# A one-core sandwich kernel: gathers and scatters of the expert rows at longer distances

## The chip, the cores and the metric

The kernel runs on one core of one Trainium2 chip. The metric is the device time of one execution in microseconds (us); the runs shown are summed up by their median. A core has five engines that the text names as the profile does: PE (TensorE; PEld is its weight load), DVE (VectorE), ACT (ScalarE), POOL (GpSimd) and SP (SyncE, which here only issues DMAs). The indirect DMAs, gathers and scatters with a list of row numbers, are issued by POOL.

## The reference

The input is x of 8 x 512 tokens of 128 numbers. Two blocks stand around it, each as x = x + layernorm(block(layernorm(x))). The first block is a Nystrom attention with a graph part (16,384 edges). The second, which the change touches, is a mixture of 16 experts, 4 of them for each token:

```
diff = x[:, :, None, :] - keys
logits = -sum(diff * diff) + x @ rw.T + rb            # [b, l, 16]
topv, topi = top_k(logits, 4);  w = softmax(topv)
hidden  = gelu(x @ w1[e].T + b1[e])                   # 128 -> 512, for each expert
exp_out = hidden @ w2[e].T + b2[e]                    # 512 -> 128
fused   = sum over the 4 chosen of w * exp_out
```

Everything is float32.

## The kernel before

**Stages.** The first 230 us or so of an execution are the attention, the graph part, the router logits of the first half of the tokens and their sorting. The rest is the expert stage. The 4096 tokens are 32 token tiles of 128, in two halves of TS = 16 tiles. Each token of a half appears four times, once for each chosen expert, so a half has JT = TS * TOPK = 64 *row tiles* of 128 rows, sorted by expert. A row tile can hold rows of more than one expert, so a half takes NI = 64 + 15 = 79 *steps*, each with one expert's weights; IALL = 158 steps in all, numbered 0 to 157. `step_of(n)` (L338) is the step of row tile n: n for the first half, n + 15 for the second (tile 64 is step 79).

**One step.** In step i, PE runs `up(i)` (L2135 to L2142: 8 matmuls, two for each of 4 chunks in float32), transposes the next row tile if one is due (`rows_T`, L2130 to L2133), then runs `down(i - 1)` (L2144 to L2150: 8 matmuls). ACT runs `gelu(i)` (L879 to L885: 4 activations), which waits for `up_ps`, the count that PE raises at the end of each `up`, and copies the transposed tile (L891). DVE runs `y_add(i - 2)` (L1657 to L1665), which waits for `down_ps` and raises `y_ready`, and for every fourth row tile `bring` (L1641 to L1655). SP loads the expert's weights (L462), four steps ahead at most.

**What POOL does in the expert stage.** For each row tile n, `rows(n)` (L585 to L594) gathers 128 rows from DRAM (L592), and `results(n)` (L596 to L602) scatters the finished tile of 128 rows to DRAM (L600): 128 gathers and 128 scatters, in one instruction order on one queue. A gather waits until `up` of the step NEAR = 8 before its own is done, and for its buffer (XR = 24 buffers, and the landing of the gather 12 before). A scatter of tile m waits for `y_ready` of step_of(m) + 16. The order is written out in L607 to L624: gather n first, from n = 27 on followed by scatter n - 27 (BEHIND); at the end of the first half scatters 37 to 50 alone; then gathers 64 to 76, each followed by scatter 51 to 63 (BEHIND_2 = 13); then gathers 77 to 90 alone; then from gather 91 on each followed by a scatter, 27 behind; at the end scatters 101 to 127. PE transposes tile n five steps before step_of(n), by `brought` (L345 to L348), except the first five tiles of the second half, 64 to 68, which are due at steps 72 to 76 and tile 69 at 79.

**The second half's row list.** Beside the steps of the first half, the second half's tokens are routed and sorted (`prepare` on DVE, ACT and PE). For each of its 16 token tiles DVE makes two one-hot tables (`tile_hots` L1456 to L1461, `lane_hots` L1463 to L1469), ACT one more (`hot_lanes` L819 to L825), and PE multiplies them (`table` L2067 to L2075) one step later. `hots_of(i)` (L351 to L353) says which token tile is due at step i: two in every three steps from step 44 to 67. At LIST_STEP = 69 DVE copies the finished list of row numbers from the PSUM (`row_list`, L1471 to L1474) and raises `idx_ready`, for which POOL waits ahead of gather 64. The same work for the first half is done ahead of the expert stage.

Of the kernel before, what the change touches and what calls it, by code (L numbers as in the profile page):

```python
# [5 lines left out]
def sandwich_kernel(nc, dense, adj_rows, adj_cols, adj_vals, wq, wk, wv_w, wv_b, qkv_w, wq_t, wk_t, out_w, out_b,  # L6
# [10 lines left out]
    P = 128  # L17
# [25 lines left out]
    TS = T // S  # L43
    JT = TS * TOPK
# [3 lines left out]
    RING = 8  # L48
    SLOTS = 32
    LEAD = 3  # L50
    BEHIND = 27
    GRP = 4
    XR = 24
    NEAR = 8
    XSEM = 12
    WR = 4
    BEHIND_2 = 13
# [5 lines left out]
    with ctx:  # L63
        def sb(name, shape, dt=fp32):
            return ctx.enter_context(nc.sbuf_tensor(name, shape, dt))

        def sem(name):
            return ctx.enter_context(nc.semaphore(name))
# [99 lines left out]
        kres = sb("kres", [P, NT, QK])  # L168
        ksp = sb("ksp", [P, NT, NS, QK], bf16)

        idx_i = sb("idx_i", [P, 2, EC], i32)
        idx_f = sb("idx_f", [P, 2, EC])
        neg = sb("neg", [P, EC])
# [145 lines left out]
        w1_in = [sem(f"w1_in{s}") for s in range(WR)]  # L319
        yk_in, pool_done = [sem(f"yk_in{i}") for i in range(3 + len(YCUTS) - 1)], sem("pool_done")  # L320
        out_ready, out_done = sem("out_ready"), sem("out_done")

        block = ctx.enter_context(nc.Block())

# [6 lines left out]
        def freed(eng, sem, count):  # L331

            if count > 0:
                eng.wait_ge(sem, count)
# [3 lines left out]
        def step_of(n):  # L338
            return n // JT * NI + n % JT
# [10 lines left out]

        def hots_of(i):  # L351
            j = i - HOT_STEP
            return TS + j // 3 * 2 + j % 3 if 0 <= j < 3 * TS // 2 and j % 3 < 2 else None  # L353

        HOT_STEP, LIST_STEP = 44, 69

# [32 lines left out]
        def act_lane(t):  # L389
            return t < LANES_ACT or t >= TS  # L390
# [17 lines left out]
        def hot_slot(t):  # L408
            return t if t < TS else t % HB[1]
# [88 lines left out]
        def _(pool):  # L498
# [83 lines left out]
                .then_inc(gates_ready, 1)  # L582


            def rows(n):  # L585
                if n >= NEAR:
                    pool.wait_ge(up_ps, step_of(n) - NEAR + 1)
                if n >= XR:
                    pool.wait_ge(own_ready, 3 * ((n - XR) // GRP) + 1)
                if n >= XSEM:  # L590
                    pool.wait_ge(xg_in[n % XSEM], 16 * (n // XSEM))
                pool.indirect_dma_start(out=xg[:, n % XR, :], out_offset=None, in_=xd[n // JT][:, :],  # L592
                                        in_offset=bass.IndirectOffsetOnAxis(ap=idx_src[:, n:n + 1], axis=0))\
                    .then_inc(xg_in[n % XSEM], 16)  # L594

            def results(m):  # L596
                pool.wait_ge(y_ready, step_of(m) + E)
                if m >= RING:
                    pool.wait_ge(y_out[m % RING], 16 * (m // RING))
                pool.indirect_dma_start(out=yd[:, :],  # L600
                                        out_offset=bass.IndirectOffsetOnAxis(ap=idx_dst[:, m:m + 1], axis=0),
                                        in_=yg[:, m % SLOTS, :], in_offset=None).then_inc(y_out[m % RING], 16)  # L602
# [1 line left out]
            pool.wait_ge(pool_done, POOL_PRE)  # L604
            pool.wait_ge(idx_ready, 1)
            pool.wait_ge(xd_done, 16)
            for n in range(JT):  # L607
                rows(n)
                if n >= BEHIND:
                    results(n - BEHIND)  # L610
            for m in range(JT - BEHIND, JT - BEHIND_2):
                results(m)
            pool.wait_ge(idx_ready, 2)
            pool.wait_ge(xd_done, 32)
            for n in range(JT, JT + BEHIND_2):
                rows(n)
                results(n - BEHIND_2)
            for n in range(JT + BEHIND_2, JT + BEHIND):
                rows(n)
            for n in range(JT + BEHIND, JALL):  # L620
                rows(n)
                results(n - BEHIND)
            for m in range(JALL - BEHIND, JALL):
# [299 lines left out]
        def _(dve):  # L923
# [342 lines left out]
            def some_stats(src, t0, t1, last):  # L1266
                for t in range(t0, t1):
                    ins = v.bn_stats(stats[:, t, :], src[:, t, :])
                step(ins)
                for t in range(t0, t1):  # L1270
                    ins = v.bn_aggr(mv[:, t, :], stats[:, t, :])  # L1271
                if last:
                    ins.then_inc(stat_ready, 1)
# [182 lines left out]
            def tile_hots(t0, n):  # L1456
                h, s = t0 // TS, hot_slot(t0)
                v.tensor_tensor(out=hot_tile[h][:, s:s + n, :, :].rearrange("p a k n -> p (a k) n"),
                                in0=iota_r[:, 0:JT].unsqueeze(1).broadcast_to([P, n * TOPK, JT]),
                                in1=tile_of[:, t0 % TS:t0 % TS + n, :].rearrange("p t k -> p (t k)").unsqueeze(2)  # L1460
                                .broadcast_to([P, n * TOPK, JT]), op=ALU.is_equal).then_inc(hot_ready, 1)  # L1461

            def lane_hots(t):  # L1463
                h, s = t // TS, t % HB[t // TS]
                freed(dve, hot_used, t - HB[h] + 1)
                for k in range(TOPK - act_lane(t)):
                    ins = v.tensor_scalar(hot_lane[h][:, s, k, :], iota_r[:, 0:P], lane[:, t % TS, k:k + 1],  # L1467
                                          code[:, t:t + 1], ALU.is_equal, ALU.mult)
                ins.then_inc(hot_ready, 1)  # L1469
# [52 lines left out]
            def normal(to, of, t, last):  # L1522
                ins = v.tensor_scalar(to, of, rstd[:, t:t + 1], nmr[:, t:t + 1], ALU.mult, ALU.add)
                if t % NT == NT - 1:
                    ins.then_inc(last, 1)

            def prepare(i):
                if 25 <= i < 25 + TS:
                    normal(xrow[:, i - 25, 0:D], x[:, TS + i - 25, :], TS + i - 25, xn_ready)
                if 1 <= i <= 6:  # L1530
                    t = TS + min(3 * (i - 1), 12 + 2 * (i - 5))
                    some_stats(xn, t, t + (3 if i < 5 else 2), i == 6)
                elif 7 <= i <= 9:
                    root(1, i - 7, 3, EPS / 4)
                elif i == 10:
                    shifts(1)
                elif 11 <= i <= 19:
                    t = TS + 2 * (i - 11)
                    if i < 19:
                        second_x(t, t + 2)  # L1540
                    if i > 11:
                        some_stats(x, t - 2, t, i == 19)
                elif 20 <= i <= 22:
                    root(1, i - 20, 4, EPS)
                elif i == 24:
                    norm_2(1)
                    square_norm(1)
                    logits_1(1)
                elif i == 25:
                    logits_2()  # L1550
                elif i == 26:
                    logits_3(1)
                elif i == 27:
                    highest()
                elif i == 28:
                    lowered()
                    highest_at(0, 4)
                elif i in (29, 30):
                    highest_at(4 + 6 * (i - 29), 10 + 6 * (i - 29))
                elif i == 31:  # L1560
                    step(v.tensor_copy(topf[:, 0:TS, :], topi[:, :, 0:TOPK]))
                    one_hots(0, 2)
                elif i == 32:
                    one_hots(2, TOPK)
                elif i == 33:
                    chosen_experts()
                elif i == 34:
                    dve.wait_ge(chosen_ready, 2)
                    dve.wait_ge(xd_done, 16)
                    targets(1)  # L1570
                elif i == 36:
                    counts(1)
                elif i == 37:
                    starts()
                elif i in (38, 39):
                    position_1(2 * (i - 38), 2 * (i - 37))
                elif i in (40, 41):
                    position_2(2 * (i - 40), 2 * (i - 39))
                elif i == 42:
                    lanes_and_tiles()  # L1580
                elif i == HOT_STEP + 2:
                    gates_1(1)
                elif i == HOT_STEP + 5:
                    gates_2(1)
                elif i == HOT_STEP + 8:
                    after_start()
                elif i == HOT_STEP + 11:
                    experts_of(1)
                elif i == HOT_STEP + 14:
                    step_experts()  # L1590
                elif i == HOT_STEP + 17:
                    expert_row(1)
                elif i == LIST_STEP:
                    row_list(1)
                if hots_of(i):
                    tile_hots(hots_of(i), 1)
                    lane_hots(hots_of(i))


            def finish(i):  # L1600
# [625 lines left out]
```

## Time and profile before

| what | value |
|---|---|
| median of 3 runs | 700.9 us (699.55 to 707.57) |
| span of the profiled execution | 694.4 us |
| PE busy | 536.4 us, 77% |
| POOL busy | 281.1 us, 40% |
| ACT busy | 353.7 us, 51% |
| DVE busy | 364.9 us, 53% |
| first gather starts | 229.56 us into the span |
| last scatter starts | 664.6 us into the span |

The span runs from the first to the last instruction of one profiled execution; its own device time is not shown apart, so the 6.5 us between the span and the median of the runs stand for what lies around it. The busy shares are means over stages with different limits: in the first 230 us POOL is mostly idle, in the expert stage it issues the indirect DMAs.

### The profile page before, as it was taken

Reading aid. Unit: us, or ns where it says so; the run is one execution under the profiler, and the core shown is the slowest. Engines: PE = TensorE matmul, PEld = TensorE weight load, DVE = VectorE, ACT = ScalarE, POOL = GpSimd, SP = SyncE. Lnnn points to the kernel's source line nnn. Section 1 sums busy time; section 2 is a strip of 40 time slices with the busy share of each in tenths; the row PEclk is TensorE's granted clock in tenths of the full one; section 3 lists DMA queues with packets and bytes.
Section 4 is the critical chain, followed back from the end, with each engine's and each line's share of the span. In section 5 each row is a group of like instructions: output and inputs, shape, how many; then the busy total and the mean of one; then the engine's idle time right before and its main releaser. Section 6 shows DMA issues by size and latency. Waiting matters only on the chain.

```text
span 694.4 us, 19926 instructions
## 1 busy us (share of the span) xinstructions
PE 536.4 (77%) x6242; PEld 481.6 (69%) x6242; DVE 364.9 (53%) x1325; ACT 353.7 (51%) x1079; POOL 281.1 (40%) x308
## 2 busy tenths in 40 slices
PE   4999879994502789977678789789977776679984
PEld 4967779993401489976677679678967776668942
DVE  6554779997999356545434553112334432233126
ACT  6524167775556365546445667336634434335513
POOL 4000000000451543566666743664566666645520
PEclk9999999998655799999999999999999989989998
DMA  8970000006001455444444645445866644546553
GB/s 229 255 280 9 3 3 0 0 0 243 1 1 76 120 161 157 138 131 131 131 140 143 204 124 162 135 144 146 264 207 180 183 130 133 145 122 192 174 197 122
DMA packets 55746, 92.28 MB, mean 133 GB/s; under 512 B 10352, under 2 KB 26096, under 8 KB 55152
## 3 DMA queue, kind: packets, MB, share of 16 engines
q1 hardware_dynamic: 45424, 72.35, 35.0%
q0 software_dynamic: 10240, 18.89, 9.2%
q8 instruction: 44, 0.72, 0.4%
q14 instruction: 38, 0.31, 0.1%
HBM read 78.07 MB, written 17.37 MB: 137 GB/s over the span
## 4 chain that ended last, share of the span: by engine, by line
PE 43%; issue 18%; DVE 18%; POOL 8%; ACT 7%; DMA 2%; DVEq 2%; another core or an unknown queue 0%; POOLq 0%; SPq 0%; ACTq 0%
PE bank L2148 15%; PE bank L2141 13%; POOL yd L600 6%; ACT value L883 3%; DVE shared L1187 2%; DVE shared L1179 2%; POOL shared L592 2%; DVE early L1467 2%; PE bank L1735 2%; DMA shared<-yd 1%; PE bank L1772 1%; PE bank L1840 1%; PE bank L1762 1%; PE bank L2133 1%; PE bank L2089 1%
## 5 line engine op out<-in xcount | busy, mean ns | idle before, releaser
L883 ACT ACTIVATE value<-bank,shared 128x128 f32<-128x128 f32 x632 | 180.8, 376 | 203.0 <-PE bank L2141 156.7
L2148 PE MATMUL bank<-shared,value 128*128 x1264 | 182.7, 290 | 62.4 <-ACT value L883 41.7
L2148 PEld LDWEIGHTS bank<-shared,value 128*128 128x128 f32 x1264 | 161.7, 200 | 76.7 <-issue 76.1
L2141 PE MATMUL bank<-early,shared 128*128 x1264 | 180.9, 288 | 5.3 <-issue 2.8
L592 POOL DMA_INDIRECT shared<-xd,early x128 | 125.5, 980 | 127.5 <-PE bank L2141 79.8
L2141 PEld LDWEIGHTS bank<-early,shared 128*128 128x128 f32 x1264 | 162.6, 200 | 9.3 <-issue 8.4
L1663 DVE SCALAR_TENSOR_TENSOR early<-bank,value,early 128x128 f32 x158 | 55.4, 351 | 195.8 <-PE bank L2148 116.6
L600 POOL DMA_INDIRECT yd<-early x128 | 128.3, 1002 | 67.8 <-DVE early L1663 36.2
L560 POOL TENSOR_TENSOR shared<-shared,xn 128x512 f32<-128x512 f32 x4 | 5.1, 1264 | 174.9 <-DVE xn L1262 167.1
L2133 PE MATMUL bank<-ident,shared 128*128 128x128 f32 x128 | 35.9, 284 | 9.0 <-DMA shared<-xd,early 5.7
L2003 PE MATMUL bank<-ksp,shared 128*128 128x32 bf16 x1536 | 40.9, 177 | 0.0
L2003 PEld LDWEIGHTS bank<-ksp,shared 128*128 128x128 bf16 x1536 | 40.0, 96 | 0.1
L891 ACT ACTIVATE early<-bank 128x128 f32<-128x128 f32 x128 | 38.4, 304 | 2.5 <-PE bank L2133 2.0
L2013 PE MATMUL bank<-xnT,shared 128*128 128x96 bf16 x512 | 24.3, 206 | 7.2 <-DVE xnT L1206 7.2
L1741 PE MATMUL bank<-zeros 128*128 128x512 bf16 x61 | 17.3, 444 | 15.0 <-DVE mv L1271 13.0
L1645 DVE TENSOR_TENSOR value<-shared,mask 128x128 f32<-128x128 f32 x16 | 4.7, 292 | 45.9 <-PE bank L2133 40.7
L2013 PEld LDWEIGHTS bank<-xnT,shared 128*128 128x128 bf16 x512 | 22.4, 98 | 8.4 <-issue 6.2
L2133 PEld LDWEIGHTS bank<-ident,shared 128*128 128x128 f32 x128 | 18.9, 148 | 11.9 <-DMA shared<-xd,early 7.4
L1187 DVE TENSOR_SCALAR shared<-iota_r,idx_f 128x512 bf16<-128x512 f16 x90 | 24.9, 345 | 0.4 <-PE bank L2013 0.4
L1179 DVE TENSOR_SCALAR shared<-shared,iota_c 128x1024 bf16 x56 | 23.3, 478 | 0.0
L1741 PEld LDWEIGHTS bank<-zeros 128*128 128x128 bf16 x61 | 6.4, 109 | 23.7 <-DVE mv L1271 13.1
L753 ACT ACTIVATE xnT<-iota_r,idx_f 128x512 f16<-128x512 f16 x32 | 21.1, 707 | 0.0
(334 smaller groups left out, 689.3 us busy)
## 6 DMA issues: line engine op xcount, KB each, us to landing
shared<-w1b SPq DMA_DIRECT2D x158, 258.0 KB
w1b<-in_w_t SPq DMA_DIRECT2D x1, 4096.0 KB, 17.8
shared<-col_dram SPq DMA_DIRECT2D x1, 4096.0 KB, 13.4
shared<-in_w_t SPq DMA_DIRECT2D x1, 4096.0 KB, 12.3
att<-yd SPq DMA_DIRECT2D x8, 512.0 KB
shared<-yd SPq DMA_DIRECT2D x4, 1024.0 KB, 9.1
xd<-xnT SPq DMA_DIRECT2D x2, 1280.0 KB
shared<-xd,early POOLq DMA_INDIRECT x128
```

The lines of the kernel that those rows point to most:

```text
L592: pool.indirect_dma_start(out=xg[:, n % XR, :], out_offset=None, in_=xd[n // JT][:, :], in_offset=bass.IndirectOffsetOnAxis(ap=idx_src[:, ...
L600: pool.indirect_dma_start(out=yd[:, :], out_offset=bass.IndirectOffsetOnAxis(ap=idx_dst[:, m:m + 1], axis=0), in_=yg[:, m % SLOTS, :], in_ ...
L883: ins = act.activation(hT[:, i % 2, tok(c)], bank[2 + i % 2][:, tok(c)], ACT.Gelu, bias=w1_now[:, i % WR, F + c:F + c + 1])
L891: act.activation(xgT[:, n % SLOTS, :], bank[n % 2][:, 0:P], ACT.Copy).then_inc(xgT_ready, 1)
L1179: ins = v.tensor_scalar(oh_c[:, s, c, :], colb[:, bass.ds(g * (EG * P), EG * P)], iota_c[:, c:c + 1], None, ALU.is_equal)
L1187: ins = v.tensor_scalar(oh_r[:, s, j, :], iota_r[:, :], idx_f[:, 0, bass.ds(g * EG + j, 1)], None, ALU.is_equal)
L1663: v.scalar_tensor_tensor(out=y, in0=bank[6 + i % 2][:, 0:P], scalar=own_f[:, bass.ds(at * (2 * E) + e, 1)], in1=y, op0=ALU.mult, op1=ALU.a ...
L2003: ins = mm(bank[s][:, j * QK:(j + 1) * QK], oh_c[:, s, c, j * P:(j + 1) * P], ksp[:, c, n, :], start=(c == 0 and n == 0), stop=(c == NT - ...
L2013: ins = mm(bank[4][:, c * NS * QK:(c + 1) * NS * QK], oh_r[:, s, j, tok(c)], kvs[:, s, j, :, :].rearrange("p n q -> p (n q)"), start=False ...
L2133: nc.tensor.transpose(bank[n % 2][:, 0:P], xg[:, n % XR, 0:D], ident[:, :]).then_inc(xgT_ps, 1)
L2141: ins = mm(bank[2 + i % 2][:, tok(c)], w1_now[:, i % WR, tok(c)], x_now, start=True, stop=True)
L2148: ins = mm(bank[6 + i % 2][:, 0:D], hT[:, i % 2, tok(c)], w2_sb[:, bass.ds(e, 1), c, :] .rearrange("p a d -> p (a d)"), start=(c == 0), st ...
```

## The change

Six things are changed, and nothing of what is computed:

1. NEAR goes from 8 to 16: a gather waits for the `up` of the step 16 before its own.
2. BEHIND goes from 27 to 34: scatters stand 34 gathers behind in the order.
3. A `pause` is added: POOL writes a scratch tile (`pause_to`, 128 x 64 float32) with a memset and waits for the memset's own semaphore. It stands behind each gather that has no scatter behind it: gathers 0 to 33 and 77 to 97.
4. The loop over the first half's gathers is written as two loops, which for the order of gathers and scatters is the same as before but for the value of BEHIND.
5. The second half's one-hot tables are made at one token tile a step, steps 44 to 59, with the lane tables ahead of the tile tables on DVE.
6. `row_list(1)` moves from step 69 to step HOT_STEP + TS + 2 = 62. LIST_STEP itself stays 69 and still sets `brought`, the steps at which PE transposes.

```
-    BEHIND = 27
+    BEHIND = 34
-    NEAR = 8
+    NEAR = 16
+        pause_to = sb("pause_to", [P, P // 2])
+        paused = sem("paused")
         def hots_of(i):
             j = i - HOT_STEP
-            return TS + j // 3 * 2 + j % 3 if 0 <= j < 3 * TS // 2 and j % 3 < 2 else None
+            return TS + j if 0 <= j < TS else None
+            def pause():
+                pool.memset(pause_to[:, :], 0.0).then_inc(paused, 1)
+                pauses[0] += 1
+                pool.wait_ge(paused, pauses[0])
-            for n in range(JT):
+            for n in range(BEHIND):
                 rows(n)
-                if n >= BEHIND:
-                    results(n - BEHIND)
+                pause()
+            for n in range(BEHIND, JT):
+                rows(n)
+                results(n - BEHIND)
 ...
             for n in range(JT + BEHIND_2, JT + BEHIND):
                 rows(n)
+                pause()
 ...
-                elif i == LIST_STEP:
+                elif i == HOT_STEP + TS + 2:
                     row_list(1)
                 if hots_of(i):
+                    lane_hots(hots_of(i))
                     tile_hots(hots_of(i), 1)
-                    lane_hots(hots_of(i))
```

## Rows read from the trace of the kernel before

**Rows 1.** The page's line of busy time, share of the span and instructions of each engine.
```profile
PE 536.4 (77%) x6242; PEld 481.6 (69%) x6242; DVE 364.9 (53%) x1325; ACT 353.7 (51%) x1079; POOL 281.1 (40%) x308
```

**Rows 2.** Stretches, `up` matmuls alone (x8 a step): start:end, length, busy, clock, DMA share, GB/s.
```profile
237.80:282.30 44.50, 20.59 (x152) 18.44 (x152) 1.00 0.55 148
282.30:372.10 89.80, 35.20 (x240) 31.56 (x240) 0.94 0.47 135
372.10:409.90 37.80, 15.20 (x96) 12.80 (x97) 0.95 0.54 165
409.90:429.80 19.90, 11.13 (x80) 9.76 (x81) 1.00 0.56 158
429.80:473.40 43.60, 17.07 (x120) 15.63 (x121) 0.96 0.49 143
473.40:498.30 24.90, 12.70 (x96) 11.78 (x96) 1.00 0.69 200
498.30:586.70 88.40, 35.10 (x240) 31.78 (x241) 0.92 0.61 177
586.70:622.70 36.00, 12.49 (x80) 11.43 (x81) 0.91 0.45 129
622.70:661.00 38.30, 21.46 (x160) 19.42 (x160) 1.00 0.61 172
```

**Rows 3.** The same view for POOL: busy time and instructions in two of the stretches.
```profile
282.30:372.10 89.80, 58.32 (x58) 0.94 0.47 135
473.40:498.30 24.90, 11.82 (x13) 1.00 0.69 200
```

**Rows 4.** Timeline of steps 39 and 40: start, length, engine, line, idle before and releaser.
```profile
341.15 1.06 PE L2141 MATMUL bank<-early,shared 128*128 x8
341.66 0.97 POOL L592 DMA_INDIRECT shared<-xd,early  x1 [0.30 <-issue]
342.94 1.49 POOL L600 DMA_INDIRECT yd<-early  x1 [0.30 <-issue]
344.97 1.14 ACT L883 ACTIVATE value<-bank,shared 128x128 f32<-128x128 f32 x4 [3.60 <-remote]
345.20 0.97 POOL L592 DMA_INDIRECT shared<-xd,early  x1 [0.78 <-PE bank L2141]
```

**Rows 5.** Timeline of step 93, with gathers alone.
```profile
488.83 1.06 PE L2141 MATMUL bank<-early,shared 128*128 x8
489.93 1.14 ACT L883 ACTIVATE value<-bank,shared 128x128 f32<-128x128 f32 x4 [0.59 <-PE bank L2141]
490.16 0.98 POOL L592 DMA_INDIRECT shared<-xd,early  x1 [0.95 <-PE bank L2141]
```

**Rows 6.** Timeline of ACT and DVE at a one-hot table of the second half.
```profile
419.58 0.99 DVE L1467 TENSOR_SCALAR xnT<-iota_r,att,code 128x128 f16<-128x128 f16 x3
420.52 0.42 ACT L822 ACTIVATE xnT<-iota_r,att 128x128 f16<-128x128 f16 x1
420.97 0.49 ACT L824 ACTIVATE xnT<-xnT,code,ncode 128x128 f16<-128x128 f16 x1
```

**Rows 7.** Timeline at step 72: gather 64 and the transpose of tile 64.
```profile
431.77 0.99 POOL L592 DMA_INDIRECT shared<-xd,early  x1 [6.79 <-issue]
435.46 0.33 PE L2133 MATMUL bank<-ident,shared 128*128 128x128 f32 x1 [2.77 <-DMA shared<-xd,early]
```

**Rows 8.** Timeline of the start: the last gather of the first burst, and `gelu(1)`.
```profile
240.35 0.95 POOL L592 DMA_INDIRECT shared<-xd,early  x1 [0.30 <-issue]
242.96 1.14 ACT L883 ACTIVATE value<-bank,shared 128x128 f32<-128x128 f32 x4 [2.42 <-PE bank L2141]
```

**Rows 9.** POOL's timeline: a memset waited for, what follows it, and the first gather.
```profile
0.81 0.20 POOL L506 MEMSET ident<- 128x128 f32 x1 [0.29 <-POOLq L2219]
1.26 0.28 POOL L507 TENSOR_SCALAR_AFFINE_SELECT ident<-ident 128x128 f32<-128x128 f32 x1 [0.24 <-POOL ident L506]
229.56 1.73 POOL L592 DMA_INDIRECT shared<-xd,early  x1 [13.04 <-issue]
```

More of the change, by code:

```diff
@@ L582, in _ @@
                 .then_inc(gates_ready, 1)
+            pauses = [0]
+            def pause():
+                pool.memset(pause_to[:, :], 0.0).then_inc(paused, 1)
+                pauses[0] += 1
+                pool.wait_ge(paused, pauses[0])
             def rows(n):
```

## The prediction

> **What bounds the kernel now.** The first thing to read is that no engine is full: PE is busy for 77% of the span and POOL for 40% [rows 1]. So I cut the expert stage into stretches by what POOL does in them, and counted steps by the `up` matmuls, 8 to a step [rows 2]. The nine stretches hold 19, 30, 12, 10, 15, 12, 30, 10 and 20 steps, 158 together, and cost per step:
>
> - gathers alone (steps 0 to 18): 44.5 / 19 = 2.34 us; the second half's (86 to 97): 24.9 / 12 = 2.08;
> - a gather and a scatter each step (19 to 48): 89.8 / 30 = 2.99; in the second half (98 to 127): 88.4 / 30 = 2.95;
> - the end of such a phase and the scatters left over from it (49 to 60): 37.8 / 12 = 3.15; in the second half (128 to 137): 36.0 / 10 = 3.60;
> - scatters alone (61 to 70): 1.99; (138 to 157, with the tail): 1.92;
> - the boundary of the halves (71 to 85): 43.6 / 15 = 2.91.
>
> PE has the same 16 matmuls in each step. What makes a step one microsecond dearer is that gathers and scatters stand together. The next view shows how [rows 4]. `up(39)` ends at 341.15 + 1.06 = 342.21, but ACT, which waits for PE's counts alone, starts its gelu at 344.97, and POOL's next gather, which waits for the same count, is released at 345.20. PE's count reaches the others 2.8 us late. Meanwhile POOL runs gather and scatter with 0.30 us between them; the count comes 0.5 us after the scatter (342.94 + 1.49 = 344.43) ends. Where POOL idles 0.95 us between gathers, gelu follows `up` by 489.93 - 489.89 = 0.04 us [rows 5]. I call this a *hold*: while POOL issues indirect DMAs back to back, what PE has finished is made known late. Its cause I can't read; that it goes with unbroken runs I can. A pair takes 0.97 + 0.30 + 0.99 + 0.30 = 2.56 us of POOL [rows 4], more than the 2.08 us of a step with gathers alone, so runs stay unbroken until POOL has to wait for PE. Over 30 steps POOL is busy 58.3 of 89.8 us, against 11.8 of 24.9 without scatters [rows 3].
>
> **The change, part by part.** Its sum is made against the span of 694.4 us and the 6.5 us between it and the median of 700.9; the profiled execution's own device time is not shown, so I take it as the median.
>
> *Distances.* A gather with its number n may go once `up(n - 16)` is done, a scatter behind it once `y_add(n - 19)` is. So gather 34 with scatter 0 goes at step 19, and the phase of pairs is steps 19 to 48 (gathers 34 to 63) in place of about 20 to 56, and 98 to 127 (gathers 98 to 127) in place of 99 to 135: 30 pairs twice where there were 37. All 128 gathers and 128 scatters remain. The 14 pairs that are parted turn into scatters alone.
>
> *Steps 49 to 60* (37.8 us before). Ten of them (49 to 58) still transpose a tile and now always make a one-hot table. ACT then has 1.14 (gelu), 0.3 (copy of the tile) and 0.42 + 0.49 [rows 4, 6], 2.35 us less small overlaps: I take 2.3. DVE's three lane tables of 0.99 [rows 6] and its other work of the step stay below that by about as much. Two steps without either are 1.9. Leftover scatters: at the last pair only about two are due, against four or more before, since the gather's wait stood 7 steps ahead and the scatter's 11, and now 15 and 18. I allow 2.5 us for one last hold. Sum: 23.0 + 3.8 + 2.5 = 29.3, gain **8.5**.
>
> *Steps 61 to 85* (19.9 + 43.6 = 63.5 before). Gather 64 stands behind scatter 50, which needs `y_add(65)`, and behind the row list, now copied at step 62. So it starts near step 68, not at the release of 72, and tile 64 is transposed at step 72: about 4 steps between, where there was none. Before, PE waited 2.77 us for it, 3.7 us after its issue [rows 7], and for tiles 66 to 68 less each. But thirteen pairs stay, and the hold with them: 13 x 2.95 = 38.4; the other 12 steps at 1.9 to 2.0, 23.1. Sum 61.5, gain **2.0**. The row list moves past one POOL wait only; the second half's rows are stored by SP at step 56, as before, and its weight loads keep their waits.
>
> *Steps 86 to 127.* As before, but step 98 now has a pair: **-1.0**.
>
> *Steps 128 to 137* (36.0 before). Scatters alone, 10 x 1.92 = 19.2, and 2.5 for the last hold: 21.7, gain **14.3**.
>
> *Pauses.* 55 of them. A memset and its wait take 1.26 - 0.81 = 0.45 us from start to start [rows 9]; the tile written here is half as wide. A gather so takes about 1.25 + 0.35 = 1.6 us of POOL. In a step with gathers alone POOL idles 0.95 us [rows 5], which hides it. Not hidden is the start: 16 gathers may now go without a wait from PE, where 8 did. Bounds: about nothing, if the pauses break the run (the eighth gather comes 7 x 0.35 = 2.5 us later, and the hold up to 242.96 [rows 8] falls away); or a hold until the burst ends. Before, the ninth gather started at 240.35 and gelu(1) at 242.96, 2.6 later [rows 8]; gather 15 would start at 229.6 + 2.4 + 14 x 1.6 = 254.4 [rows 9], so gelu(1) at 257: 14 us later. I take zero, since a broken run is nearer to [rows 5], and keep 14.
>
> *One-hot tables at one a step*: the tables themselves are counted above; after step 60 the old ones fall away (inside the 1.9). The order lane before tile on DVE: both are counted before the matmul starts, nothing. Scratch tile, semaphore: nothing.
>
> Sum: 8.5 + 2.0 - 1.0 + 14.3 = 23.8. Span 670.6, **time 677 us**.
>
> **The skill against it.** The trace shows a gather stretched to 1.73 us [rows 9] and a scatter to 1.49 [rows 4], where 0.97 to 0.99 is usual. The Trainium skill, SBUF — State Buffer, section "SBUF: two separate sides", calls the port pair of GpSimd and VectorE an exclusive lock: the pauses' writes could then wait for a DVE operation, or hold one up. That speaks against the pauses; no row shows such a wait of a memset in the expert stage. The rule for the dear pause below is in the Trainium skill too, GPSIMD Engine Reference, section "Instruction dispatch": an instruction completes when all eight cores are done, and this gates only who waits for its semaphore. By it a pause ends with the gather's descriptors and not with its landing, which would strike the last rival out; no row here shows it.
>
> **The rivals.**
>
> *POOL becomes the bound and the hold shrinks.* With eight more steps of lead the pairs could run at 2.56 us: 73 pairs x 0.39 = 28 us more, 649 us. Against it: POOL catches up with its waits whatever the lead is, and then has to wait for PE again.
>
> *The start is held.* 14 us as above, and up to 4 more where gathers 77 to 81 become free together near step 81: 691 to 695 us. For it: gelu(1) was late behind a burst already [rows 8].
>
> *The pause is dear.* If each gather behind a memset took the 1.73 us of the first one [rows 9], a gather would need 2.7 us, more than a step. Gather 33 would land, 3.7 us after its issue [rows 7], near 229.6 + 33 x 2.7 + 3.7 = 322.4; tile 33 is due at step 28, now at 282.3 + 9 x 2.99 = 309.2 [rows 2]: 13 us. In the second half 21 gathers take 56.7 us where the 25 steps until tile 97 is due take about 49: 8 us. 698 us.
>
> *The pause waits for the landing; the one on the slower side.* Then a gather with its pause takes 3.7 [rows 7] + 0.4 = 4.1 us. First half 33 x 4.1 + 229.6 + 3.7 - 309.2 = 59, second 21 x 4.1 - 49 = 37: 773 us at the most. It decides for slower from 54 t - 125 = 31, which is t = 2.9 us for a gather and its pause. Against it: memsets in the trace end in 0.2 us and are waited out in 0.24 more; but none stands behind an indirect DMA.
>
> **How the numbers follow.** A change of 1% (7 us) is about what can be told from none: 693.9 and 707.9. Forecast 0.66, POOL bound 0.05, start held 0.14, pause dear 0.07, waiting for the landing 0.08. Half of the held start ends near 695 and counts within 1%, as does the dear pause: faster 0.78, same 0.14, slower 0.08. The forecast's own range is 662 to 690 (last holds of 0 to 5 us each, ACT's 2.3 between 2.0 and 2.6, the boundary's gain 0 to 7). The range over the cases is 660 to 698; it leaves out 649 and what lies beyond 698.
>
> **What would show it.** After the change gathers and scatters should stand together in 73 steps at 2.9 to 3.0 us, and steps 49 to 60 and 128 to 137 should cost 2.2 to 2.5; PE's waits for gather 64 should be gone; gather-to-gather distance in the first burst about 1.6 us. If gelu(1) starts after 250, the start is held. If PE waits for gathers around step 28, the pause is dear. The forecast is wrong in its core if scatters alone, now earlier, cost 3 us a step too.

## The result, and the profile after

The changed kernel takes 709.7 us (705.7 to 717.9, 19 runs) where the kernel before takes 701.6 (699.5 to 707.6, 19 runs): a ratio of 1.0111, with a 95% interval of 1.0086 to 1.0137. It is slower by 8 us; 677 was forecast. The profiled execution has a span of 707.9 us against 694.4, 13.5 more; a second trace of the same kernel (`f1_after_b` below) has 702.7, so some of these 13.5 us belong to the one execution. The trace of the kernel before is also a quick one: in every run of the record that lists both, the span is 1.7 to 2.0 us shorter than the device time, not 6.5, so that execution took about 696 us, some 5 below the median (an estimate from these spans).

The page of the changed kernel, its busy line, to lay beside [rows 1]:

```profile
PE 539.5 (76%) x6240; PEld 489.0 (69%) x6242; DVE 364.1 (51%) x1325; ACT 355.5 (50%) x1079; POOL 291.4 (41%) x363
```

The work is the same but for 55 memsets on POOL (308 instructions became 363). Time went into waits, so the stretches have to be compared. These are the changed kernel's, cut at the same steps and with the same columns as [rows 2]:

```profile
237.50:293.10 55.60, 21.43 (x152) 19.29 (x152) 0.91 0.47 131
293.10:385.30 92.20, 35.17 (x240) 31.83 (x240) 0.94 0.46 133
385.30:419.40 34.10, 14.21 (x96) 12.16 (x96) 0.95 0.52 162
419.40:443.20 23.80, 11.51 (x80) 10.71 (x81) 0.87 0.56 156
443.20:497.10 53.90, 18.70 (x120) 17.64 (x121) 0.80 0.41 116
497.10:521.60 24.50, 12.67 (x96) 11.74 (x96) 1.00 0.67 201
521.60:612.90 91.30, 35.81 (x240) 32.40 (x241) 0.93 0.59 173
612.90:637.30 24.40, 11.57 (x80) 10.53 (x80) 0.93 0.53 149
637.30:676.00 38.70, 21.32 (x160) 19.46 (x160) 1.00 0.63 180
```

Five rows moved by more than 3 us. Steps 0 to 18 cost 55.6 us instead of 44.5, steps 61 to 85 cost 23.8 + 53.9 = 77.7 instead of 63.5, and against that steps 49 to 60 gave 3.7 back and steps 128 to 137 gave 11.6. Where 11 us went in the first row, the changed kernel's timeline says (start, length, engine, line, what it did, idle time before it and who ended it; lines are picked here and in the timelines below):

```profile
241.54 1.09 PE L2153 MATMUL bank<-early,shared 128*128 x8
...
243.86 0.17 POOL L590 MEMSET pause_to<- 128x64 f32 x1
244.23 1.08 PE L2153 MATMUL bank<-early,shared 128*128 x8
244.30 0.95 POOL L601 DMA_INDIRECT shared<-xd,early  x1 [0.27 <-POOL pause_to L590]
245.69 0.95 POOL L601 DMA_INDIRECT shared<-xd,early  x1 [0.27 <-issue]
...
252.10 1.14 ACT L895 ACTIVATE value<-bank,shared 128x128 f32<-128x128 f32 x4 [9.14 <-remote]
...
255.43 0.95 POOL L601 DMA_INDIRECT shared<-xd,early  x1 [0.27 <-issue]
257.64 1.91 PE L2153 MATMUL bank<-early,shared 128*128 x8
258.05 1.14 ACT L895 ACTIVATE value<-bank,shared 128x128 f32<-128x128 f32 x4 [3.52 <-remote]
```

The first line is `up(2)`; it ends at 242.63. ACT, which waits for PE alone, starts `gelu(2)` at 252.10, 9.5 us later. `up(3)` ends at 245.31 and `gelu(3)` starts at 258.05, 12.7 us later; `up(4)`, which stands behind `down(2)` and so behind `gelu(2)`, starts only at 257.64. All that time POOL issues gathers 1.39 us apart (0.95, the memset's 0.17, 0.27 of waiting), 19 of them from 229.6 to 255.4. I call such a row of indirect DMAs, with at most a pause between two of them, a *run*, and NEAR, the number of steps that a gather may be ahead, its *lead*: this is the run that the lead of 16 allows. Step 3 takes 13.4 us. The same again at the boundary, where gathers 77 to 81 follow the last pair:

```profile
475.50 1.06 PE L2153 MATMUL bank<-early,shared 128*128 x8
476.72 0.99 POOL L601 DMA_INDIRECT shared<-xd,early  x1 [0.30 <-issue]
477.39 1.06 PE L2153 MATMUL bank<-early,shared 128*128 x8
477.70 0.18 POOL L590 MEMSET pause_to<- 128x64 f32 x1
478.15 0.97 POOL L601 DMA_INDIRECT shared<-xd,early  x1 [0.27 <-POOL pause_to L590]
...
482.34 0.95 POOL L601 DMA_INDIRECT shared<-xd,early  x1 [0.27 <-issue]
484.41 1.14 ACT L895 ACTIVATE value<-bank,shared 128x128 f32<-128x128 f32 x4 [8.63 <-remote]
```

This is `gelu(81)`, 484.41 - 476.56 = 7.9 us behind the end of `up(81)` (the first line), and it starts 1.1 us after the last gather of the run has ended (483.29). Steps 69, 77 and 82 take 6.1, 8.3 and 10.5 us. The granted clock of the stretch is 0.80, between the two levels of 1.2 and 2.4 GHz, where it was 0.96 [rows 2]; PE's `up` is busy for 18.7 us instead of 17.1, so the waits are the larger part.

### The profile page after: what moved, and what is told of

Its sections match the earlier page's. It is cut to its first block, busy times and chain, and to the rows that moved or that the text cites. A ratio compares the mean times of both kernels' runs of the same rounds, so it can differ in the third digit from the quotient of the medians.

```text
span 707.9 us, 20013 instructions
## 1 busy us (share of the span) xinstructions
PE 539.5 (76%) x6240; PEld 489.0 (69%) x6242; DVE 364.1 (51%) x1325; ACT 355.5 (50%) x1079; POOL 291.4 (41%) x363
## 3 DMA queue, kind: packets, MB, share of 16 engines
q1 hardware_dynamic: 45424, 72.35, 34.7%
## 4 chain that ended last, share of the span: by engine, by line
PE 38%; DVE 18%; issue 17%; POOL 8%; another core or an unknown queue 7%; ACT 7%; DVEq 3%; DMA 2%; POOLq 0%; SPq 0%; ACTq 0%
PE bank L2160 13%; PE bank L2153 10%; POOL yd L609 6%; ACT value L895 2%; DVE shared L1199 2%; DVE shared L1191 2%; DVE early L1479 2%; POOL shared L601 2%; DMA shared<-yd 1%; PE bank L1747 1%; DVE early L1675 1%; DVEq L1675 1%; PE bank L1852 1%; PE bank L1784 1%
## 5 line engine op out<-in xcount | busy, mean ns | idle before, releaser
L2160 PE MATMUL bank<-shared,value 128*128 x1264 | 187.6, 295 | 72.7 <-ACT value L895 43.8
L2160 PEld LDWEIGHTS bank<-shared,value 128*128 128x128 f32 x1264 | 167.3, 206 | 84.9 <-issue 84.2
L2153 PEld LDWEIGHTS bank<-early,shared 128*128 128x128 f32 x1264 | 165.8, 204 | 6.6 <-issue 6.1
L609 POOL DMA_INDIRECT yd<-early x128 | 130.2, 1017 | 89.8 <-DVE early L1675 65.0
L765 ACT ACTIVATE xnT<-iota_r,idx_f 128x512 f16<-128x512 f16 x32 | 21.1, 707 | 0.0
```

Of the source, the lines that this page charges most:

```text
L609: pool.indirect_dma_start(out=yd[:, :], out_offset=bass.IndirectOffsetOnAxis(ap=idx_dst[:, m:m + 1], axis=0), in_=yg[:, m % SLOTS, :], in_ ...
L2153: ins = mm(bank[2 + i % 2][:, tok(c)], w1_now[:, i % WR, tok(c)], x_now, start=True, stop=True)
L2160: ins = mm(bank[6 + i % 2][:, 0:D], hT[:, i % 2, tok(c)], w2_sb[:, bass.ds(e, 1), c, :] .rearrange("p a d -> p (a d)"), start=(c == 0), st ...
```

## The experiments

**Two levels.** The same two kernels do not always stand in this relation. In some comparisons the kernel before takes 699 to 702 us and in others 642 to 645, with all kernels of one comparison on the same level. I call the first *held* and the second *free*, for in the free ones PE's counts are not late anywhere: in all eight free traces no gelu starts more than 0.5 us after its `up` has ended and ACT is free, and in each of the twelve held ones 37 to 58 of the 158 do. One chip number came up with both levels, so I can't say what the level belongs to. The result above is a held one. The expectations of `e1_nopause` to `e4_ramp` were written before the free level was known, for the held one, and those four runs came out free; what they say of the held level is tested by later runs. Ratios are only compared within a level, and this table of stretches (us, from the starts of `up`) is read the same way; sum is steps 0 to 156.

```
steps      before after f1   f2   f3   f4   e6    e8   g3   g4   h1  | free: e3   a1
0-3          9.8  20.0 20.3 21.1  8.8  8.9  22.8  8.8 13.1  8.8  9.6 |      8.8   8.8
4-18        34.7  35.5 35.2 33.9 34.9 34.8  34.1 39.1 40.7 42.7 34.8 |     34.9  35.2
19-33       43.5  46.2 46.2 44.3 55.7 37.9  59.9 47.8 46.2 44.8 44.7 |     34.7  35.0
34-48       46.3  46.0 45.9 47.4 47.6 47.9  49.2 47.2 45.9 47.4 47.1 |     42.4  35.9
49-60       37.7  34.1 31.6 31.3 30.1 48.0  34.4 29.0 31.8 31.6 40.4 |     33.4  28.3
61-70       20.0  23.9 21.4 22.6 21.5 19.7  20.6 22.1 18.5 18.5 18.5 |     18.0  18.0
71-85       43.6  53.9 55.1 53.5 50.2 44.3  59.1 45.9 45.6 44.4 45.6 |     38.7  30.4
86-97       24.9  24.5 24.5 24.5 24.5 24.6  24.5 30.7 37.3 34.3 24.6 |     25.5  24.8
98-127      88.4  91.3 92.2 91.8 93.7 84.7 107.3 94.2 91.2 91.2 93.4 |     74.3  63.9
128-137     36.0  24.4 24.1 25.9 24.6 43.9  27.6 26.0 24.5 26.3 35.9 |     25.0  22.5
138-156     37.1  36.0 34.2 36.1 34.7 36.0  38.6 34.8 34.9 34.8 36.0 |     34.3  34.8
sum          422   436  431  432  426  431   478  425  430  425  431 |      370   338
```

**The changed kernel itself, twice more.** `a1_after` and `f1_after_b` are the changed kernel, unedited.

> The changed kernel itself, unaltered, beside the kernel before, for comparison with the four variants. Where PE's counts are not held back during POOL's bursts (gelu 0.04 us behind up in the steps of pairs), theory A expects it faster than before by 3 to 4%: the bursts are harmless, pairs cost some 2.4 us a step. Where they are held back (gelu 2 to 3 us behind up in the steps of pairs of the kernel before), it is slower by about 1%, with 12 us lost at the start and 10 near step 82.

Measured, free: 612.4 us against 645.5, ratio 0.9529 (0.9444 to 0.9613), more than the 3 to 4% that was expected there. Its busy line and three of its stretches (steps 0 to 18, 19 to 48, 98 to 127):

```profile
PE 510.8 (84%) x6242; PEld 463.6 (76%) x6242; DVE 363.9 (60%) x1325; ACT 357.7 (59%) x1079; POOL 288.8 (47%) x363
```

```profile
238.50:282.50 44.00, 21.94 (x152) 19.84 (x153) 0.96 0.59 164
282.50:353.40 70.90, 32.94 (x240) 29.11 (x240) 1.00 0.61 171
...
454.90:518.80 63.90, 32.64 (x241) 29.21 (x242) 1.00 0.80 237
```

POOL runs the very same burst at the start, and here nobody waits for it. Its timeline:

```profile
245.15 0.95 POOL L601 DMA_INDIRECT shared<-xd,early  x1 [0.27 <-POOL pause_to L590]
245.43 1.06 PE L2153 MATMUL bank<-early,shared 128*128 x8
246.53 1.14 ACT L895 ACTIVATE value<-bank,shared 128x128 f32<-128x128 f32 x4 [0.53 <-PE bank L2153]
246.54 0.95 POOL L601 DMA_INDIRECT shared<-xd,early  x1 [0.27 <-POOL pause_to L590]
```

The gelu follows `up` by 246.53 - 246.49 = 0.04 us in the middle of the burst. So every hold read here stands beside a run of indirect DMAs, but a run does not make a hold by itself. In the free trace the 30 steps of the pairs cost 70.9 us, 2.36 each, though a pair still takes POOL 2.56: PE draws on the lead of 16 while POOL falls behind. With the lead of 8 that reserve ends half way (`e3_hots`, 34.7 and then 42.4 us for 15 steps each).

> The changed kernel itself, beside its own variants. Two regimes are known by now: on some chips PE's counts reach the others at once and the kernel before takes 642 to 645 us; on others they are held back while POOL issues indirect DMAs close together, and it takes 699 to 702. Where they are held: ratio 1.00 to 1.02, with steps 0 to 3 at 20 us and one step of about 10 us near step 82. Where they are not: ratio 0.95, as measured there once (612.4 against 645.5).

Measured, held: 710.8 us against 701.0, ratio 1.0143 (1.0063 to 1.0224); steps 0 to 3 took 20.3 us, step 83 took 8.5. The first result repeats.

**The pauses.** `e1_nopause`, `e5_nopause_b` and `f2_nopause_c` are the changed kernel without them:

```diff
             for n in range(BEHIND):
                 rows(n)
-                pause()
...
             for n in range(JT + BEHIND_2, JT + BEHIND):
                 rows(n)
-                pause()
```

> The changed kernel without its 55 pauses behind gathers. Theory A (what counts is how closely the indirect DMAs follow each other, and for how many): the start's gathers come 1.25 us apart instead of 1.39, still held; steps 0 to 3 take 18 to 20 us and the boundary as long as with pauses or 1 to 2 us less, ratio to the kernel before 1.00 to 1.02. Rival B (a pause's wait is itself what lets the counts be held, a semaphore more in the same queue): steps 0 to 3 fall to 10 us, ratio 0.98. Rival C (the pause does break the hold in part): steps 0 to 3 over 22 us and the steps 4 to 18 longer, ratio 1.03. On a chip that holds nothing: 0.95, as measured (611.1).

Measured: held 712.1 us, ratio 1.0167 (1.0089 to 1.0244), steps 0 to 3 at 21.1 us, a little over the 18 to 20 of theory A. Free: 610.3, 0.9519 (0.9404 to 0.9634), and, beside `a1_after`, 611.1, 0.9503 (0.9416 to 0.9589). The pauses do nothing that can be measured at either level; `e5_nopause_b`, for which 1 to 2% over the changed kernel was expected at the free level, is 0.2% faster. Theory A (the spacing of the indirect DMAs and their number decide) stands: 1.25 us between gathers is held like 1.39. Doubled pauses, `e2_pause2` and `f3_pause2_b` (`pause()` twice in each place):

> The changed kernel with each pause doubled: gathers come about 1.83 us apart where nothing else is waited for. Theory A by spacing: if 1.83 us between two indirect DMAs is enough for PE's counts to get through, steps 0 to 3 fall from 20 us to under 12 and the singles stay as they are, 10 us below the changed kernel (ratio about 0.99 to 1.00 where counts are held). Rival (the hold ends only when POOL has nothing left to issue for about a microsecond): steps 0 to 3 last 16 gathers of 1.83 us, 24 to 27 us, ratio 1.02 or more. On a chip that holds nothing: 0.985, as measured (634.7).

Measured: held 706.5 us, ratio 1.0082 (1.0038 to 1.0126); free 634.7, 0.9854 (0.9743 to 0.9966). Its timeline at the start:

```profile
246.11 0.38 POOL L590 MEMSET pause_to<- 128x64 f32 x2
246.75 0.95 POOL L601 DMA_INDIRECT shared<-xd,early  x1 [0.27 <-POOL pause_to L590]
247.91 1.06 PE L2155 MATMUL bank<-early,shared 128*128 x8
248.36 0.95 POOL L601 DMA_INDIRECT shared<-xd,early  x1 [0.27 <-issue]
249.01 1.14 ACT L897 ACTIVATE value<-bank,shared 128x128 f32<-128x128 f32 x4 [0.53 <-PE bank L2155]
```

At 1.60 us between gathers (248.36 - 246.75) the gelu is 249.01 - 248.97 = 0.04 us behind: no hold, and steps 0 to 3 fall from 20.0 to 8.8. But these slower gathers have not reached the lead of 16 when the pairs begin. POOL then runs 14 indirect DMAs with no break, and steps 25 and 26 take 11.5 and 8.0 us: steps 0 to 33 sum to 99.4 us against 101.7 with single pauses and 88.0 before. The hold moved, and the 10 us that theory A expected to gain came to 4.3 (706.5 for 710.8).

**One-hot tables and list.** `e3_hots` is the kernel before with only this part of the change:

```diff
-            return TS + j // 3 * 2 + j % 3 if 0 <= j < 3 * TS // 2 and j % 3 < 2 else None
+            return TS + j if 0 <= j < TS else None
...
-                elif i == LIST_STEP:
+                elif i == HOT_STEP + TS + 2:
...
+                    lane_hots(hots_of(i))
                     tile_hots(hots_of(i), 1)
-                    lane_hots(hots_of(i))
```

> The kernel before with the one-hot tables at one token tile a step and the row list at step 62 alone; distances and pauses as before. If the denser tables are near free beside the steps of pairs: 700 to 703 us. If they cost what a hold hides in part (ACT and DVE are fuller in steps 44 to 59): 705 or more. The earlier row list can't release gather 64, which then still waits for step 72.

Measured, free: 644.7 us, ratio 1.0043 (0.9993 to 1.0093): no difference that can be told, though not at the level that the expectation was written for. `e7_oldlist` takes the same part back from the changed kernel:

> The changed kernel with its one-hot tables and its row list as before (two in three steps, list at step 69). It tells what the earlier list is worth. Gather 64 then waits for step 69 in place of some step 68: if the boundary's gain comes from the gather's distance, it is within 0.5% of the changed kernel; if it comes from the list, 1 to 2% slower than that.

Measured, held: 711.2 us, ratio 1.0170 (1.0118 to 1.0223); its steps 49 to 60 took 29.8 us, no longer than the 29 to 34 with the denser tables, and its steps 61 to 85 took 80.1, against 77.7 and 76.5 in the two held traces of the changed kernel. Its ratio is above their 1.0111 and within the interval of their 1.0143, each from another comparison. No worth of this part shows at either level.

**The lead alone.** `e6_near16` is the kernel before with `NEAR = 16` for 8:

> The kernel before with NEAR at 16 and nothing else: 16 gathers free at the start, scatters still 27 behind, the row list still at step 69. The scatters' own wait then bounds the pairs. Where PE's counts are held back during POOL's bursts (gelu 2 to 3 us behind up in the steps of pairs), theory A expects a loss of 8 to 12 us at the start, so 1% slower or more. Where they are not, it expects a little gain, since gather 64 no longer waits for step 72: 0 to 1%.

Measured, held: 744.9 us, ratio 1.0664 (1.0599 to 1.0729), the worst of all, 46 us where 8 to 12 were expected. Steps 128 to 137 fall to 27.6, but the start costs 22.8, with one step of 15.7, and steps of 6 to 11 us stand all along the pairs. Its timeline at the boundary:

```profile
458.44 1.06 PE L2141 MATMUL bank<-early,shared 128*128 x8
461.16 0.98 POOL L592 DMA_INDIRECT shared<-xd,early  x1 [0.30 <-issue]
462.45 0.97 POOL L600 DMA_INDIRECT yd<-early  x1 [0.30 <-issue]
...
466.30 0.98 POOL L592 DMA_INDIRECT shared<-xd,early  x1 [0.31 <-issue]
468.98 1.40 ACT L883 ACTIVATE value<-bank,shared 128x128 f32<-128x128 f32 x5 [8.96 <-remote]
```

A run of nine indirect DMAs, the first four of them before 461.16, and `gelu(71)` 468.98 - 459.50 = 9.5 us late.

**The scatters' distance alone.** `f4_behind34` is the kernel before with `BEHIND = 34` for 27:

> The kernel before with BEHIND 27 made 34 and nothing else: NEAR stays 8, no pauses, old one-hots, row list at 69. It keeps the part of the change that takes pairs away and leaves out the longer lead of the gathers, which by the theory is what makes POOL issue 16 gathers unbroken at the start and after the boundary. Expected where counts are held: steps 0 to 3 at 10 us as before, 49 to 60 shorter by 4 to 8 us, 128 to 137 shorter by about 11, boundary unchanged: 680 to 688 us, ratio 0.97 to 0.98. Rival (the gain at 128 to 137 comes from the longer lead and not from the scatters' distance): ratio 0.995 to 1.00. On a chip that holds nothing the singles with lead 8 take 2.1 to 2.4 us a step as the pairs' 2.5 fall away for 7 steps twice: ratio 0.99.

Measured, held: 714.8 us, ratio 1.0197 (1.012 to 1.0275). The main expectation, 680 to 688, failed, and the rival named for it holds. Fewer pairs do help while they last (steps 19 to 33: 37.9 for 43.5), but at their end the lead of 8 leaves 34 - 8 = 26 steps between last gather and its scatter instead of 19, and the scatters left over go in one run. Its timeline:

```profile
397.16 0.97 POOL L600 DMA_INDIRECT yd<-early  x1 [0.30 <-issue]
398.93 1.06 PE L2141 MATMUL bank<-early,shared 128*128 x8
...
407.38 0.97 POOL L600 DMA_INDIRECT yd<-early  x1 [0.30 <-issue]
407.49 0.37 PE L2141 MATMUL bank<-early,shared 128*128 x1 [1.02 <-issue]
408.93 0.37 PE L2141 MATMUL bank<-early,shared 128*128 x1 [1.06 <-issue]
...
410.51 1.14 ACT L883 ACTIVATE value<-bank,shared 128x128 f32<-128x128 f32 x4 [6.18 <-PE bank L2141]
```

Nine scatters stand in this run, and `gelu(57)` is 410.51 - 399.99 = 10.5 us late. PE itself is late here: the eight matmuls of `up(58)`, between which the program has no wait, take 5.3 us (from 404.97) instead of the usual 1.1 to 2.1. `up(54)` of `h1_near12` below shows the same, 4.4 us. Scatters alone hold too: steps 49 to 60 cost 48.0 us and 128 to 137 cost 43.9. The changed kernel gains at these two places with lead and distance together (34 - 16 = 18). The distance alone loses there; the lead alone (`e6_near16`, 27 - 16 = 11) gains 3.3 and 8.4 us there and loses more elsewhere.

**Raising the lead gently.** `e4_ramp` and `e8_ramp_mid16` are the changed kernel with a lead that climbs from 8 to 16 over the single gathers (e4: with lead 8 for the 13 paired gathers of the boundary; e8: with 16 there):

```diff
-                if n >= NEAR:
-                    pool.wait_ge(up_ps, step_of(n) - NEAR + 1)
+                if n >= 8:
+                    pool.wait_ge(up_ps, step_of(n) - lead(n) + 1)
```

> The changed kernel with the lead of the gathers grown from 8 to 16 over gathers 8 to 34 and 77 to 98, and 16 for gathers 64 to 76. Where counts are held, theory A expects both bursts' holds gone, 20 us less than the changed kernel (680 to 692 us where before is 701). Where they are not, it is within 1% of the changed kernel, and 1 to 2% faster than the same ramp with a lead of 8 for gathers 64 to 76 (0.975 of before).

Measured: e4 free 625.8 us, ratio 0.9748 (0.9646 to 0.985); e8 held 704.0, 1.0071 (1.0029 to 1.0114), where 680 to 692 was expected. The 13 us step is gone (8.8 for steps 0 to 3), and against the kernel before 4.4 us come back in steps 4 to 18 and 5.8 in steps 86 to 97, where each pair of gathers close together is held. Steps 61 to 85 take 68.0 us although the 13 paired gathers keep the lead of 16: 4.5 more than before, where the changed kernel, whose gathers 77 to 81 follow at once, takes 14.2 more.

**Wider spacing by a little.** `g1_gap156` and `g3_gap156_b` are one kernel, `g2_gap173` and `g4_gap173_b` another: the changed kernel with pauses of two or three memsets and one wait, and lead 8 for the boundary's 13 paired gathers.

```diff
-                pool.memset(pause_to[:, :], 0.0).then_inc(paused, 1)
+                pool.memset(pause_to[:, 0, :], 0.0)
+                pool.memset(pause_to[:, 1, :], 0.0).then_inc(paused, 1)
...
-                if n >= NEAR:
-                    pool.wait_ge(up_ps, step_of(n) - NEAR + 1)
+                near = 8 if JT <= n < JT + BEHIND_2 else NEAR
+                if n >= near:
+                    pool.wait_ge(up_ps, step_of(n) - near + 1)
```

> The changed kernel with two edits: each pause is two memsets and one wait (gathers alone come about 1.56 us apart instead of 1.39, where 1.83 let PE's counts through at the start and 1.39 held them), and the 13 gathers that are paired with scatters at the boundary keep the old lead of 8. Theory A (spacing and number of indirect DMAs in a row decide): if 1.56 is enough, steps 0 to 3 take 9 to 12 us, the lead has reached 16 before the pairs begin, so steps 19 to 33 stay at 46 (not 56 as with 1.83), and steps 71 to 85 fall from 54 to 44 to 47: 10 to 18 us under the changed kernel, ratio to the kernel before 0.975 to 0.995 where counts are held. Rival (1.56 still holds): steps 0 to 3 take 20 to 23 us and only the boundary gains, ratio 1.00 to 1.01. On a chip that holds nothing: 0.955 to 0.975.

> The same with three memsets to a pause (1.73 us), beside it. Where counts are held: steps 0 to 3 at 9 us, one unbroken run of 4 to 8 us in steps 22 to 26, boundary 44 to 47, ratio 0.98 to 1.00. Where they are not: 0.976, as measured.

The spacings came out at 1.48 and 1.56 us, not 1.56 and 1.73. Only g2's ratio fell into the range that theory A had for it. Free (g1, g2): 626.6 and 626.2 us, ratios 0.9775 (0.9743 to 0.9807) and 0.9764 (0.9735 to 0.9793); the lead of 8 costs 9 us at steps 71 to 85 there (39.4 and 39.7 against 30.4). Held (g3, g4): 708.8 and 702.8 us, ratios 1.0137 (1.0079 to 1.0196) and 1.0044 (1.0002 to 1.0087). At the start the hold came later and in smaller parts: steps 0 to 18 took 53.8 and 51.5 us, against 55.5 in the changed kernel and 44.5 before, and `gelu(3)` of g4 is 2.8 us late between gathers 1.56 us apart. The boundary's pairs are as before (45.6 and 44.4), so a lead of 8 for these 13 gathers takes their loss away, but the gathers behind them now raise the lead from 8 to 16 and are held in steps 86 and 87 (9.9 and 7.4 us in g3, 7.8 and 6.6 in g4). Steps 68 to 97 sum to 88.8 and 84.6 us, against 89.7 and 88.3 in the two traces of the changed kernel. The hold moved again and shrank by 4 to 5 us at most.

**A smaller lead.** `h1_near12`: doubled pauses, `NEAR = 12`, lead 8 in the boundary's pairs.

> The changed kernel with doubled pauses, NEAR 12 in place of 16, and lead 8 for the boundary's 13 paired gathers. Theory A (raising the lead costs a hold unless the gathers come 1.6 to 1.9 us apart, and it has to be raised before the pairs begin): by steps, where counts are held, 0 to 18 at 44, 19 to 48 at 91 with no unbroken run at step 25 (a lead of 12 is reached by gather 34, 16 was not), 49 to 60 at 33, 68 to 97 at 78, 98 to 127 at 91, 128 to 137 at 29, the rest as before: 414 against 422 before, ratio 0.985 to 0.993, the first below the kernel before. Rival (the gains at the ends of the pairs need the full lead of 16): 49 to 60 at 38 and 128 to 137 at 35, ratio 1.00 to 1.01. On a chip that holds nothing: 0.98 to 0.99.

Measured, held: 707.3 us, ratio 1.0073 (1.0037 to 1.0108), not 0.985 to 0.993. Up to step 48 the expectation holds (136.2 us against 134.3 before, no burst at step 25). The ends do not: steps 54 and 132 take 11.4 and 11.6 us, and the stretches cost 40.4 and 35.9 us, as the rival had it. POOL's timeline around step 54:

```profile
385.35 0.97 POOL L602 DMA_INDIRECT shared<-xd,early  x1 [1.50 <-remote]
386.62 1.11 POOL L610 DMA_INDIRECT yd<-early  x1 [0.30 <-issue]
...
395.83 0.97 POOL L610 DMA_INDIRECT yd<-early  x1 [0.30 <-issue]
400.38 1.01 POOL L610 DMA_INDIRECT yd<-early  x1 [3.58 <-DVE early L1678]
```

The last gather of the half is followed by eight scatters with no break, the ones left over by a distance of 34 with a lead of 12. Step 132 has the same with seven. Step 107 takes 10.5 us in a third way: doubled pauses have set the gathers 1.97 us apart while a step takes 1.90, so the lead has not grown when the pairs begin, and POOL runs ten indirect DMAs unbroken.

No version beats the kernel before where it is held. Where it is free the changed kernel does, by 4.7%, and so does it without its pauses.

## Why the prediction was wrong, step by step

**The hold itself** was read correctly from [rows 4, 5], and it decides the result. What failed is that I took it for a property of single pairs and charged each stretch for the pairs in it. The runs showed a delay that goes with the whole of a run of POOL, and a longer lead makes the runs longer.

**Pauses and start, taken as zero**: this is the step that failed first. "A broken run is nearer to [rows 5]" chose the wrong end. [Rows 5] has 0.95 us of idle POOL between gathers; a pause leaves 0.44 from gather to gather, 0.17 of it the memset. The start, a term put at nothing, cost 10.2 us (steps 0 to 3, 20.0 for 9.8), inside the bound of 14 that I kept, at 1.39 us between gathers where I forecast 1.6. Removing the pauses changed nothing, doubling them ended this hold: shown by f2 and f3. The sign named for it, `gelu(1)` after 250, was the wrong one: `gelu(1)` started at 240.46 and `gelu(2)` at 252.10.

**Steps 61 to 85, forecast 61.5 us**: measured 77.7. This is the largest error, 16 us. I counted thirteen pairs at the 2.95 of before, though their gathers' lead rises from 8 to 16 in this place too: POOL runs up to six indirect DMAs of the pairs in a row, and then gathers 77 to 81 as well. The prediction had up to 4 us for the latter in a rival and nothing for the former. g3 and g4, whose pairs with lead 8 cost what they did before, show that the lead is the cause. How the 14.2 us lost divide is less sure: `e8_ramp_mid16` keeps the lead of 16 in the pairs, parts only the gathers behind them, and loses 4.5.

**Steps 49 to 60, forecast 29.3**: measured 34.1, and 31.6 in the second trace. The mechanism is right, the last hold was larger than 2.5 us in the first trace (step 49 took 6.4).

**Steps 86 to 127, forecast -1.0**: -2.5. **Steps 128 to 137, forecast 21.7**: 24.4, a gain of 11.6 for 14.3. I had put it down to parted pairs; `f4_behind34` shows that these alone lose 7.9 us here, and `h1_near12`, with a lead of 12, gains 0.1, while the longer lead without parted pairs (`e6_near16`) gains 8.4: most of the gain is the lead's.

**The one-hot tables at nothing**: right, by e3 and e7. **The boundary's late gather**: this part came as forecast and still gained nothing. Gather 64 starts at 433.46, in step 68, and PE transposes its tile at 446.32 without a wait. But the next gelu starts only at 448.11, after 5.1 us of idle ACT, and step 72 takes 5.0 us as before: a hold stands where the wait for the gather stood.

Of the rivals *the start is held* came true, with 0.14 and 691 to 695 us; with the 16 us of the boundary added to its 691 it would have given 707. *The pause is dear* and *the pause waits for the landing* did not happen: a gather behind a memset took 0.95 us, and the pair of both 1.39. The 2.7 us for a gather in the first of them is also wrong by its own rows: 1.73 in place of 0.97 makes 1.6 into 2.4, and its 698 us into about 680. The Trainium skill, GPSIMD Engine Reference, section "Instruction dispatch", ties the completion of an instruction to the work of all eight cores. This trace agrees: the next gather starts 0.44 us after the last one has ended, memset and wait between them, while 3.7 us lay between a gather's start and the first use of its rows [rows 7]. The Trainium skill's SBUF — State Buffer, section "SBUF: two separate sides", spoke against the pauses by the port shared with VectorE; no run shows such a wait, the 55 memsets took 0.163 to 0.177 us each. *POOL becomes the bound* gave 649 us for the changed kernel, from pairs at 2.56 us. Where nothing is held it takes 612.4, its pairs 2.36 us each; that the kernel before takes 642 to 645 there, near 649, is chance.

The sum (us, seen from the kernel before; minus is a loss): steps 0 to 48 forecast 0, measured -13.4; 49 to 60 8.5 and 3.6; 61 to 85 2.0 and -14.2; 86 to 127 -1.0 and -2.5; 128 to 137 14.3 and 11.6; 138 to 156 0 and 1.1. Measured together -13.8, against 13.5 us of span; between the medians it is 8, since the trace of the kernel before is a quick one.

## What to carry to other kernels

A longer lead is not free slack: the queue that runs ahead issues its reserve in one burst, at the start, after every stretch with a shorter lead, and where a second kind of work joins in. Before lengthening one, find in the trace what is late behind the longest unbroken run, and charge the new run as a whole, not each pair in it by the mean of before. Time such a change in more than one comparison, since the sign of this one differs between them.

## What the runs showed of the hardware that was not expected

- The same kernel takes 699 to 702 us in some comparisons and 642 to 645 in others. The gather itself takes 0.95 us at both, and the same burst, 1.39 us apart, delays a gelu by 9.5 us in the one and by 0.04 us in the other.
- Where counts are held, raising the lead by 8 costs 8 to 14 us in steps 0 to 33, however the gathers are spaced: they take 88.0 us before, and 101.7, 99.3 (no pauses), 99.4 (doubled), 100.0 (1.48 us), 96.3 (1.56 us) and 95.7 (ramp). With scatters still 27 behind (`e6_near16`) it is 116.8. A lead of 12 took 89.1.
- Gathers 1.25 to 1.56 us apart are held, 1.60 us apart at the start of `f3_pause2_b` they were not. That run also had a smaller lead at the time, so the limit isn't separated from the number in a row. Nor is it separated from the kind of pause: g4 at 1.56 us has three memsets and one wait, `f3_pause2_b` at 1.60 two memsets and two waits.
- Open: what delays the counts. The runs show whom it hits (ACT, DVE and POOL behind PE, and twice PE within an `up`), when it ends (1.1 us after the run's last gather at 483.29, earlier within long runs: 252.10), and that it is absent at one level. Why, none of them tells. The ends of matmuls in the profile are modelled, so a matmul that ends late and a count that comes late look the same here. What the two levels belong to is open too.
